# Recurrent blocks of a graph network: TensorE's order of sums, transposes and gate products within a group

## The chip, the cores and the metric

The kernel runs on one core of a Trainium2 chip. The metric is the device time of one execution in microseconds; the time before is the median of three runs. The profile shows one further execution, whose times are those of the hardware profiler.

## What is computed

The program is a network of four graph layers over 3125 nodes (padded to 3200, 25 tiles of 128) and 100000 edges. The change touches the third layer alone, four recurrent blocks one after the other:

```python
for b in range(4):
    x = h * norm_src[:, None]
    agg = segment_sum(x[src], dst, num_segments=n)
    g = agg * norm_dst[:, None] @ gcn_w[b] + gcn_b[b]
    gi = g @ gru_w_ih[b].T + gru_b_ih[b]
    i_r, i_z, i_n = split(gi, 3, axis=-1)
    h_r, h_z, h_n = split(gru_b_hh[b], 3)
    r = sigmoid(i_r + h_r)
    z = sigmoid(i_z + h_z)
    h = relu((1.0 - z) * tanh(i_n + r * h_n))
```

After the last block its input is added and each row is normalized.

## The kernel before

`gru_block` (from line 1395) makes one block. A matrix AT of edge counts between nodes, in bf16, stays in SBUF; the sum over neighbours is a product of the node features with it. At the start of a block `Split` loads the features in five pieces, scales them and writes them as three bf16 parts each (ScalarE and VectorE in turns).

The nodes are then handled in NG = 5 groups of GT = 5 tiles, 640 columns, each in two halves of HW = 320 columns. For each group, TensorE's loop does in this order (lines 1442 to 1457):

- it waits until VectorE has taken the rows of the prior group out of the two banks `pa` (semaphore `taken`);
- it sums the neighbours of half 0 into `pa[0]` and of half 1 into `pa[1]`: `sum_neighbours`, 25 tiles x 3 parts = 75 matmuls of 320 columns each (line 350);
- per half it multiplies the scaled sums by the weights `wg` into `pg[2]` (line 1448, f32), once VectorE has scaled them (line 1491, `sums_out`);
- it waits until ScalarE has added the bias to both halves (line 1466, `convs_out`) and makes six gate products, three gates x two halves, into the six banks `pg` (line 1452, f32);
- it waits for the state and transposes it, five f32 transposes into `pa` (line 1456).

ScalarE makes the bias, the sigmoids of the reset gate and of the keep gate (lines 1469 and 1472) and the tanh (line 1474). VectorE scales the sums, mixes reset gate and candidate (line 1498), makes the state (line 1502) and copies the transposed rows into `r_y` (line 1513; in the last block line 1515 adds the residual and the norm follows, with a square root on ScalarE, line 1477). SyncE stores `r_y` (line 1435) and, in the last block, loads the residual into it first (line 1433). All four engines run loops over the five groups. Each engine works its queue in order, and the semaphores say what it waits for. In the profile an f32 product stands as two records.

Of the kernel before, what the change touches and what calls it, by code (L numbers as in the profile page):

```python
# [12 lines left out]
P = 128  # L13
# [18 lines left out]
GT = 5  # L32
NG = NT // GT
GW = GT * P
HW = GW // 2
# [8 lines left out]
ALU = mybir.AluOpType  # L44
ACT = mybir.ActivationFunctionType
AX_X = mybir.AxisListType.X
ds = bass.ds
# [296 lines left out]
def sum_neighbours(pe, AT, parts, banks, f, g, half, lo):  # L344

    for j in range(NT):
        if half == 0 and j % GT == 0:
            pe.wait_ge(lo, f * NG + j // GT + 1)
        for k in range(SPLIT):
            mm = pe.matmul(banks, parts[:, k, j, f * P:(f + 1) * P], AT[:, j, ds(g * GW + half * HW, HW)],  # L350
                           start=(j == 0 and k == 0), stop=(j == NT - 1 and k == SPLIT - 1))
    return mm
# [1039 lines left out]
GATES = 3  # L1392


def gru_block(nc, K, D, AT, b, source, from_scale, to_scale, parts, target, residual):

    with ExitStack() as ctx:
        m = Mem(nc, ctx)
        wg = m.sb("r_wg", [P, P])
# [6 lines left out]
        summed, conv, reset, keep, cand = (work[:, i, :] for i in range(NG))  # L1406
        split = Split(m, source, 1, parts, [work[:, i, :].rearrange("p (t c) -> p t c", c=P) for i in range(NG)], from_scale)
# [3 lines left out]
        pa = [m.ps(f"r_pa{i}", [P, BANK]) for i in range(2)]  # L1411
        pg = [[m.ps(f"r_pg{c}{i}", [P, BANK]) for i in range(2)] for c in range(GATES)]
# [5 lines left out]
        halves = [slice(i * HW, (i + 1) * HW) for i in range(2)]  # L1418
        with nc.Block() as block:
            @block.sync  # L1420
            def _(sp):
                sp.sem_inc(stored, 16)
                for i in range(NG):
                    split.load(sp, i)
                sp.dma_start(wg[:, :], D["gcn_w"][b * P:(b + 1) * P, :]).then_inc(weights, 16)
                sp.dma_start(wi[:, :], D["gru_w"][b * P:(b + 1) * P, :]).then_inc(weights, 16)
                sp.dma_start(bg[:, :], D["gcn_b"][b * P:(b + 1) * P, :]).then_inc(weights, 16)
                sp.dma_start(bi[:, :], D["gru_bi"][b * P:(b + 1) * P, :]).then_inc(weights, 16)
                sp.dma_start(bh[:, :], D["gru_bh"][b * P:(b + 1) * P, :]).then_inc(weights, 16)
                with sp.Fori(0, NG) as g:  # L1430
                    if residual is not None:
                        sp.wait_ge(stored, g * 16 + 16)
                        sp.dma_start(y[:, :, :], rows(residual, g * GT, GT)).then_inc(resid, 16)
                    sp.wait_ge(done, g + 1)
                    sp.dma_start(rows(target, g * GT, GT), y[:, :, :]).then_inc(stored, 16)
                sp.wait_ge(stored, 16 * NG + 16)

            @block.tensor
            def _(pe):
                pe.sem_inc(turned, 1)  # L1440
                pe.wait_ge(weights, 80)
                with pe.Fori(0, NG) as g:
                    pe.wait_ge(taken, g * GT + 1)
                    for i in range(2):
                        sum_neighbours(pe, AT, parts, pa[i][:, 0:HW], 0, g, i, split.lo).then_inc(sums, 1)
                    for i in range(2):
                        pe.wait_ge(sums_out, g * 2 + i + 1)
                        pe.matmul(pg[2][i][:, 0:HW], wg[:, :], summed[:, halves[i]], start=True, stop=True).then_inc(convs, 1)
                    pe.wait_ge(convs_out, g * 2 + 2)
                    for c in range(GATES):  # L1450
                        for i in range(2):
                            pe.matmul(pg[c][i][:, 0:HW], wi[:, c * P:(c + 1) * P], conv[:, halves[i]],
                                      start=True, stop=True).then_inc(gates, 1)
                    pe.wait_ge(state, g + 1)
                    for u in range(GT):
                        pe.transpose(pa[u // 4][:, u % 4 * P:(u % 4 + 1) * P], cand[:, u * P:(u + 1) * P],
                                     K["identf"][:, :]).then_inc(turned, 1)

            @block.scalar
            def _(act):  # L1460
                split.scalar(act)
                act.wait_ge(biases, 1)
                with act.Fori(0, NG) as g:
                    for i in range(2):
                        act.wait_ge(convs, g * 2 + i + 1)
                        act.activation(conv[:, halves[i]], pg[2][i][:, 0:HW], ACT.Identity, bias=bg[:, 0:1]).then_inc(convs_out, 1)
                    for i in range(2):
                        act.wait_ge(gates, g * 6 + i + 1)
                        act.activation(reset[:, halves[i]], pg[0][i][:, 0:HW], ACT.Sigmoid, bias=brz[:, 0:1]).then_inc(gates_out, 1)
                    for i in range(2):  # L1470
                        act.wait_ge(gates, g * 6 + 3 + i)
                        act.activation(keep[:, halves[i]], pg[1][i][:, 0:HW], ACT.Sigmoid, bias=brz[:, 1:2], scale=-1.0).then_inc(gates_out, 1)
                    act.wait_ge(mixed, g * 2 + 2)
                    act.activation(cand[:, :], cand[:, :], ACT.Tanh, bias=bi[:, 2:3]).then_inc(tanned, 1)
                    if residual is not None:
                        act.wait_ge(var, g + 1)
                        act.activation(mv[:, :, 1], mv[:, :, 1], ACT.Sqrt).then_inc(dev, 1)

            @block.vector
            def _(dve):  # L1480
                dve.sem_inc(taken, 1)
                split.vector(dve)
                dve.wait_ge(weights, 80)
                dve.tensor_tensor(brz[:, :], bi[:, 0:2], bh[:, 0:2], ALU.add)
                dve.drain()
                dve.tensor_scalar(brz[:, 1:2], brz[:, 1:2], -1.0, None, ALU.mult)
                dve.drain().then_inc(biases, 1)
                with dve.Fori(0, NG) as g:
                    for i in range(2):
                        dve.wait_ge(sums, g * 2 + i + 1)  # L1490
                        dve.tensor_tensor(summed[:, halves[i]], pa[i][:, 0:HW], to_scale[:, ds(g * GW + i * HW, HW)],
                                          ALU.mult).then_inc(sums_out, 1)
                    dve.drain()
                    dve.wait_ge(turned, g * GT + 1)
                    for i in range(2):
                        dve.wait_ge(gates_out, g * 4 + i + 1)
                        dve.wait_ge(gates, g * 6 + 5 + i)
                        dve.scalar_tensor_tensor(out=cand[:, halves[i]], in0=reset[:, halves[i]], scalar=bh[:, 2:3],
                                                 in1=pg[2][i][:, 0:HW], op0=ALU.mult, op1=ALU.add).then_inc(mixed, 1)
                    dve.wait_ge(gates_out, g * 4 + 4)  # L1500
                    dve.wait_ge(tanned, g + 1)
                    dve.scalar_tensor_tensor(out=cand[:, :], in0=cand[:, :], scalar=0.0, in1=keep[:, :],
                                             op0=ALU.max, op1=ALU.mult).then_inc(state, 1)
                    if residual is None:
                        dve.wait_ge(stored, g * 16 + 16)
                    else:
                        dve.wait_ge(resid, g * 16 + 16)
                    for u in range(GT):
                        if u in (0, 4):
                            dve.wait_ge(turned, g * GT + min(u + 4, GT) + 1)  # L1510
                        result = pa[u // 4][:, u % 4 * P:(u % 4 + 1) * P]
                        if residual is None:
                            dve.tensor_copy(y[:, u, :], result).then_inc(taken, 1)
                        else:
                            dve.tensor_tensor(y[:, u, :], result, y[:, u, :], ALU.add).then_inc(taken, 1)
                    if residual is not None:
                        dve.drain()
                        norm_stats(dve, y, stats, mv, GT).then_inc(var, 1)
                        dve.wait_ge(dev, g + 1)
                        norm_apply(dve, y, mv, GT)  # L1520
                    dve.drain()
                    dve.sem_inc(done, 1)


RBF = 64
# [580 lines left out]
```

## Time and profile before

| what | us |
|---|---|
| median of 3 runs | 6668.77 (6667.44 to 6669.37) |
| the profiled execution | 6675.19 |
| its span | 6673.6 |
| TensorE busy in the span | 4334.3 |
| four blocks, first sums to last copy | 161.7, 162.3, 163.3, 161.7 |

The profiled execution lies 6.4 us above the median. A row of the timeline gives start, length, engine, line, operation, the tiles written and read, the number of instructions merged, and in brackets the idle time before and who ended it. The ends of matmuls are modelled, so that a matmul's length reaches into the next one's time: what a stream of them costs is read from start to start. The granted clock (PEclk) is 1.00 at 2.4 GHz and 0.50 at 1.2 GHz.

### The profile page before, as it was taken

The page shows a single profiled execution, that of the slowest core. Times are in us where ns is not written, and L with a number is a line of the kernel's source. Part 1 is how long each engine was busy: PE and PEld are TensorE (multiplying, and loading weights), DVE is VectorE, ACT ScalarE, POOL GpSimd, SP SyncE. Part 2 cuts the span into 40 slices and gives each one's busy share as a digit, 9 for nine tenths or more (in the row PEclk, how much of TensorE's full clock was granted, in tenths as well). Part 3 has the DMA queues.
Part 4 walks back from the last instruction along what each step waited for, and adds up shares of the span by engine and source line. Part 5 has one row for each costly group of instructions (what it writes and reads, how often), then busy time and mean ns, then how long its engine had stood idle before and what let it go on. Part 6 is the DMA issues. An engine that isn't in the chain of part 4 may idle for free. (4 is left out here: it accounts for less than half of the span.)

```text
span 6673.6 us, 101944 instructions
## 1 busy us (share of the span) xinstructions
PE 4334.3 (65%) x26966; PEld 3026.4 (45%) x26967; DVE 3767.7 (56%) x8412; ACT 1205.4 (18%) x2011; POOL 3659.2 (55%) x3721
## 2 busy tenths in 40 slices
PE   0666667186267777775466666641888778778774
PEld 0111114154156566553355555531555556556653
DVE  8777771054589898988466666662111244444443
ACT  0111111011211111111212211110211222222221
POOL 1666664600277777772477777735000057777771
PEclk9999998598589899987577777766998888888886
DMA  4111114110244444443233333353000123222344
GB/s 198 41 44 44 41 44 177 46 33 15 64 127 116 123 122 121 117 123 75 74 81 80 79 80 83 82 114 130 11 18 21 31 64 75 74 75 74 75 71 42
DMA packets 309188, 518.20 MB, mean 78 GB/s; under 512 B 105621, under 2 KB 221727, under 8 KB 298934
## 3 DMA queue, kind: packets, MB, share of 16 engines
q0 software_dynamic: 131616, 291.86, 18.6%
q1 hardware_dynamic: 177430, 224.82, 10.3%
q8 instruction: 43, 0.70, 0.0%
q14 instruction: 99, 0.81, 0.0%
HBM read 412.95 MB, written 103.45 MB: 77 GB/s over the span
## 5 line engine op out<-in xcount | busy, mean ns | idle before, releaser
L1017 POOL DMA_INDIRECT e_ring<-att_rows,e_near x1792 | 1841.6, 1028 | 550.2 <-issue 484.2
L1770 POOL DMA_INDIRECT e_nodes<-x,e_edges x880 | 884.2, 1005 | 311.5 <-issue 274.5
L1084 PE MATMUL e_psum<-e_ring,e_whole_pick 128*128 128x264 f32 (+1 forms) x3584 | 849.5, 390 | 297.8 <-DVE e_ring L1244 288.8
L1084 PEld LDWEIGHTS e_psum<-e_ring,e_whole_pick 128*128 128x128 f32 x3584 | 649.4, 225 | 423.5 <-issue 195.7
L1039 PE MATMUL e_px<-t_parts,e_pick 128*128 x5376 | 692.9, 270 | 118.1 <-DVE e_prod L1162 56.3
L1162 DVE TENSOR_TENSOR e_prod<-e_px,e_ring 128x512 f32<-128x512 f32 x672 | 458.3, 682 | 495.9 <-DMA e_ring<-att_rows,e_near 413.3
L1688 POOL DMA_INDIRECT sorted<-bx_held,bx_index x550 | 545.0, 991 | 251.3 <-issue 248.9
L280 PE MATMUL b_acc<-b_pick_key,b_pick_lo 128*128 128x416 bf16 (+1 forms) x1960 | 504.4, 346 | 176.5 <-DVE b_pick_key L251 159.5
L350 PE MATMUL r_pa<-gru_counts,gru_parts 128*128 x3000 | 448.7, 316 | 187.3 <-DMA r_bh<-in_gru_bh 169.6
L1039 PEld LDWEIGHTS e_px<-t_parts,e_pick 128*128 128x128 bf16 x5376 | 452.6, 107 | 210.2 <-issue 139.5
L1126 ACT ACTIVATE e_whole_pick<-e_pturn 128x512 f32<-128x512 bf16 x448 | 266.5, 595 | 1324.8 <-PE e_pturn L1075 1280.5
L251 DVE TENSOR_SCALAR b_pick_key<-b_lane,b_base,b_keyf 128x800 bf16<-128x800 int16 x980 | 487.4, 497 | 0.0
L1806 PE MATMUL e_pa<-e_msg,e_pick 128*128 128x128 f32 x1768 | 315.6, 333 | 249.4 <-DVEq L1864 248.4
L1806 PEld LDWEIGHTS e_pa<-e_msg,e_pick 128*128 128x128 f32 x1768 | 264.4, 229 | 435.4 <-DVEq L1864 420.4
L350 PEld LDWEIGHTS r_pa<-gru_counts,gru_parts 128*128 128x128 bf16 x3000 | 306.7, 103 | 328.9 <-issue 193.5
L1152 DVE TENSOR_REDUCE e_dots<-e_prod 128x8 f32<-128x512 f32 (+1 forms) x672 | 453.0, 674 | 0.0
L350 PE MATMUL g_pa<-gin_counts,g_parts 128*128 x2250 | 319.6, 306 | 191.8 <-ACT g_parts L316 160.6
L1244 DVE TENSOR_TENSOR e_ring<-e_ring 128x1024 f32<-128x1024 f32 (+1 forms) x448 | 423.7, 946 | 23.7 <-issue 23.7
L250 DVE TENSOR_SCALAR b_pick_lo<-b_lane,b_lof 128x128 bf16<-128x128 int16 x980 | 264.6, 270 | 239.1 <-PE b_acc L280 194.8
L1761 POOL IOTA e_lane<- 128x128 f32 x1 | 0.2, 237 | 712.2 <-ACTq L1822 712.2
L1863 DVE TENSOR_TENSOR e_msg<-e_msg,e_nodes 128x512 f32<-128x512 f32 x220 | 153.7, 699 | 397.3 <-DMA e_nodes<-x,e_edges 395.9
L280 PEld LDWEIGHTS b_acc<-b_pick_key,b_pick_lo 128*128 128x128 bf16 x1960 | 121.5, 98 | 543.5 <-DVE b_pick_key L251 527.7
(335 smaller groups left out, 6579.9 us busy)
## 6 DMA issues: line engine op xcount, KB each, us to landing
e_relb<-place SPq DMA_DIRECT2D x56, 1024.0 KB
sorted<-o_fill SPq DMA_DIRECT2D x13, 2244.0 KB, 34.3
e_edges<-sorted SPq DMA_DIRECT2D x221, 132.0 KB
e_ring<-att_rows,e_near POOLq DMA_INDIRECT x1792
kept<-gin_counts SPq DMA_DIRECT2D x5, 4000.0 KB, 33.5
gru_counts<-kept SPq DMA_DIRECT2D x5, 4000.0 KB
bx_held<-in_edge_rows POOLq DMA_DIRECT2D x51, 363.0 KB
e_nodes<-x,e_edges POOLq DMA_INDIRECT x880
```

Of the source, the lines that this page charges most:

```text
L251: dve.tensor_scalar(pick_key[:, b, :], lane[:, :], base[:, ds(w, 1)], keyf[:, ds(c, 1)], ALU.add, ALU.is_equal).then_inc(picked, 1)
L280: mm = pe.matmul(acc[q % 2][:, h, 0:z - a], pick_lo[:, b, :], pick_key[:, b, a:z], start=False, stop=False, skip_group_check=True)
L350: mm = pe.matmul(banks, parts[:, k, j, f * P:(f + 1) * P], AT[:, j, ds(g * GW + half * HW, HW)], start=(j == 0 and k == 0), stop=(j == NT ...
L1017: pool.indirect_dma_start(out=ring[:, s, r, 0:wd + HEADS], out_offset=None, in_=xrows, in_offset=bass.IndirectOffsetOnAxis(ap=near[:, s, r ...
L1039: mm = pe.matmul(px[g % 2][:, x * wd:(x + 1) * wd], pick[:, 1 - s, r, :], parts[:, n, ds(t, 1), :].rearrange("p o c -> p (o c)"), start=(n ...
L1084: mm = pe.matmul(psum[q % 2][:, 0:RING], whole_pick[:, q % 2, c, :], ring[:, s, q * G + c, :], start=(c == 0), stop=(c == G - 1))
L1152: dve.tensor_reduce(dots[:, s, :, g * XB:(g + 1) * XB].rearrange("p h x -> p x h"), prod[:, g % 4, :].rearrange("p (x h c) -> p x h c", x= ...
L1162: dve.tensor_tensor(prod[:, g % 4, :].rearrange("p (x c) -> p x c", x=XB), px[g % 2][:, :].rearrange("p (x c) -> p x c", x=XB), ring[:, 1 ...
L1244: dve.tensor_tensor(rows_, rows_, ring[:, s, q * G:(q + 1) * G, wd:wd + HEADS].unsqueeze(3).broadcast_to([P, G, HEADS, ch]), ALU.mult).the ...
L1688: pool.indirect_dma_start(out=self.D["sorted"], in_=self.held[s][:, u, :], in_offset=None, out_offset=bass.IndirectOffsetOnAxis(ap=self.in ...
L1770: pool.indirect_dma_start(out=nodes[:, s, u, :], out_offset=None, in_=source, in_offset=bass.IndirectOffsetOnAxis(ap=edges[:, q, u, RBF + ...
L1806: mm = pe.matmul(pa[s][:, 0:P], pick[:, s, u, :], msg[:, s, u, :], start=(u == 0), stop=(u == SUB - 1))
```

## The change

TensorE's loop is put in another order. It sums half 0 of group g; transposes the state of group g-1 (`turn`), now into the two banks of `pg[0]`; multiplies half 0 by `wg`; sums half 1; multiplies half 1; waits until the rows of group g-1 are taken; then it makes the three gate products of half 0 and the three of half 1, each half after its own bias. In the first group `turn` works on a state that does not exist yet and whose result nobody reads; after the loop a last `turn` follows. ScalarE makes the sigmoids in the order reset 0, keep 0, reset 1, keep 1. VectorE's loop is written out for the five groups: scaling of half 0, the rows of the prior group (with the norm in the last block), scaling of half 1, then mixing and state.

```diff
                 with pe.Fori(0, NG) as g:
+                    sum_neighbours(pe, AT, parts, pa[0][:, 0:HW], 0, g, 0, split.lo).then_inc(sums, 1)
+                    turn(g - 1)
+                    convolve(g, 0)
+                    sum_neighbours(pe, AT, parts, pa[1][:, 0:HW], 0, g, 1, split.lo).then_inc(sums, 1)
+                    convolve(g, 1)
                     pe.wait_ge(taken, g * GT + 1)
                     for i in range(2):
-                        sum_neighbours(pe, AT, parts, pa[i][:, 0:HW], 0, g, i, split.lo).then_inc(sums, 1)
-                    for i in range(2):
-                        pe.wait_ge(sums_out, g * 2 + i + 1)
-                        pe.matmul(pg[2][i][:, 0:HW], wg[:, :], summed[:, halves[i]], start=True, stop=True).then_inc(convs, 1)
-                    pe.wait_ge(convs_out, g * 2 + 2)
-                    for c in range(GATES):
-                        for i in range(2):
+                        pe.wait_ge(convs_out, g * 2 + i + 1)
+                        for c in range(GATES):
                             pe.matmul(pg[c][i][:, 0:HW], wi[:, c * P:(c + 1) * P], conv[:, halves[i]],
                                       start=True, stop=True).then_inc(gates, 1)
-                    pe.wait_ge(state, g + 1)
-                    for u in range(GT):
-                        pe.transpose(pa[u // 4][:, u % 4 * P:(u % 4 + 1) * P], cand[:, u * P:(u + 1) * P],
-                                     K["identf"][:, :]).then_inc(turned, 1)
+                turn(NG - 1)
```

The two functions that it calls:

```python
def turn(g):
    pe.wait_ge(state, g + 2)
    for u in range(GT):
        pe.transpose(pg[0][u // 4][:, u % 4 * P:(u % 4 + 1) * P], cand[:, u * P:(u + 1) * P],
                     K["identf"][:, :]).then_inc(turned, 1)

def convolve(g, i):
    pe.wait_ge(sums_out, g * 2 + i + 1)
    pe.matmul(pg[2][i][:, 0:HW], wg[:, :], summed[:, halves[i]], start=True, stop=True).then_inc(convs, 1)
```

ScalarE:

```diff
                     for i in range(2):
-                        act.wait_ge(gates, g * 6 + i + 1)
+                        act.wait_ge(gates, g * 6 + i * GATES + 1)
                         act.activation(reset[:, halves[i]], pg[0][i][:, 0:HW], ACT.Sigmoid, ...)
-                    for i in range(2):
-                        act.wait_ge(gates, g * 6 + 3 + i)
+                        act.wait_ge(gates, g * 6 + i * GATES + 2)
                         act.activation(keep[:, halves[i]], pg[1][i][:, 0:HW], ACT.Sigmoid, ...)
```

VectorE, whose steps are otherwise those of before, put into three functions:

```diff
-                with dve.Fori(0, NG) as g:
...
+                dve.sem_inc(state, 1)
+                for g in range(NG):
+                    scale_sums(g, 0)
+                    if g:
+                        take_rows(g - 1)
+                    scale_sums(g, 1)
+                    make_state(g)
+                take_rows(NG - 1)
```

`take_rows` reads `pg[0]` instead of `pa`. The loads, the splitting, the stores and the end of a block are as they were.

## Rows read from the trace of the kernel before

**Rows 1.** The page: the span, and the group of the sums' matmuls.
```profile
span 6673.6 us, 101944 instructions
...
L350 PE MATMUL r_pa<-gru_counts,gru_parts 128*128 x3000 | 448.7, 316 | 187.3 <-DMA r_bh<-in_gru_bh 169.6
```

**Rows 2.** Busy time by window, one for each of the four blocks.
```profile
core 0: us, PE busy (x) PEld busy (x) DVE busy (x) ACT busy (x) POOL busy (x), PEclk, DMA share, GB/s
4670.30:4832.00 161.70, 140.69 (x855) 93.90 (x855) 26.72 (x61) 38.13 (x55) 0.00 (x0) 0.92 0.03 8
4845.90:5008.20 162.30, 141.18 (x855) 94.02 (x855) 26.08 (x60) 26.41 (x44) 0.00 (x0) 0.92 0.03 8
5022.20:5185.50 163.30, 142.20 (x855) 94.19 (x855) 25.92 (x60) 26.28 (x44) 0.00 (x0) 0.92 0.03 8
5199.40:5361.10 161.70, 140.69 (x855) 93.92 (x855) 39.53 (x129) 45.19 (x64) 0.00 (x0) 0.92 0.06 16
```

**Rows 3.** Timeline, first group of the first block, to the next sums.
```profile
4670.35 21.89 PE L350 MATMUL r_pa<-gru_counts,gru_parts 128*128 x150 [124.95 <-DMA r_bh<-in_gru_bh]
...
4682.19 0.49 DVE L1491 TENSOR_TENSOR r_work<-r_pa,to_scale 128x320 f32<-128x320 f32 x1 [4.00 <-PE r_pa L350]
...
4692.07 0.70 PE L1448 MATMUL r_pg<-r_work,r_wg 128*128 128x320 f32 x2
4692.38 0.49 DVE L1491 TENSOR_TENSOR r_work<-r_pa,to_scale 128x320 f32<-128x320 f32 x1 [9.70 <-PE r_pa L350]
...
4692.93 0.81 PE L1448 MATMUL r_pg<-r_work,r_wg 128*128 128x320 f32 x2 [0.16 <-DVE r_work L1491]
...
4694.31 1.28 ACT L1469 ACT_TABLE_LOAD   x1
...
4694.35 3.50 PE L1452 MATMUL r_pg<-r_work,r_wi 128*128 128x320 f32 x12 [0.62 <-ACT r_work L1466]
4695.61 0.94 ACT L1469 ACTIVATE r_work<-r_pg,r_brz 128x320 f32<-128x320 f32 x2
...
4697.35 1.09 DVE L1498 SCALAR_TENSOR_TENSOR r_work<-r_work,r_bh,r_pg 128x320 f32<-128x320 f32 x2 [4.47 <-PE r_pg L1452]
4698.47 0.83 ACT L1474 ACTIVATE r_work<-r_work,r_bi 128x640 f32<-128x640 f32 x1 [1.08 <-DVE r_work L1498]
...
4699.33 0.83 DVE L1502 SCALAR_TENSOR_TENSOR r_work<-r_work 128x640 f32<-128x640 f32 x1 [0.90 <-ACT r_work L1474]
...
4700.21 1.17 PE L1456 MATMUL r_pa<-identf,r_work 128*128 128x128 f32 x5 [2.36 <-DVE r_work L1502]
4701.20 1.08 DVE L1513 COPY r_y<-r_pa 128x128 f32<-128x128 f32 x5 [1.05 <-PE r_pa L1456]
...
4702.43 22.89 PE L350 MATMUL r_pa<-gru_counts,gru_parts 128*128 x150 [1.05 <-DVE r_y L1513]
```

**Rows 4.** Windows of 1 us in that group; columns as in rows 2.
```profile
4697.00:4698.00 1.00, 0.85 (x4) 0.26 (x2) 0.65 (x2) 0.39 (x1) 0.00 (x0) 1.00 0.00 0
...
4699.00:4700.00 1.00, 0.00 (x0) 0.00 (x0) 0.67 (x1) 0.98 (x2) 0.00 (x0) 1.00 0.00 0
...
4701.00:4702.00 1.00, 0.38 (x2) 0.00 (x0) 0.80 (x4) 0.00 (x0) 0.00 (x0) 0.50 0.00 0
```

**Rows 5.** Timeline of TensorE, second group's end, and the last block's groups.
```profile
4733.31 0.77 PE L1456 MATMUL r_pa<-identf,r_work 128*128 128x128 f32 x5 [2.36 <-DVE r_work L1502]
4735.23 21.87 PE L350 MATMUL r_pa<-gru_counts,gru_parts 128*128 x150 [1.15 <-DVE r_y L1513]
...
5199.43 21.88 PE L350 MATMUL r_pa<-gru_counts,gru_parts 128*128 x150 [14.91 <-DMA r_bh<-in_gru_bh]
...
5329.17 21.86 PE L350 MATMUL r_pa<-gru_counts,gru_parts 128*128 x150 [1.15 <-DVE r_y L1515]
```

**Rows 6.** Timeline of SyncE, second load of the residual; DMA issues: KB, us to landing.
```profile
5238.08 0.39 SPq L1433 DMA_DIRECT2D r_y<-x  x1
...
state<-r_y SPq DMA_DIRECT2D x15, 320.0 KB, 2.5
```

More of the change, by code:

```diff
@@ L1441, in _ @@
                 pe.wait_ge(weights, 80)
-                with pe.Fori(0, NG) as g:
+                def turn(g):
+                    pe.wait_ge(state, g + 2)
+                    for u in range(GT):
+                        pe.transpose(pg[0][u // 4][:, u % 4 * P:(u % 4 + 1) * P], cand[:, u * P:(u + 1) * P],
+                                     K["identf"][:, :]).then_inc(turned, 1)
+                def convolve(g, i):
+                    pe.wait_ge(sums_out, g * 2 + i + 1)
+                    pe.matmul(pg[2][i][:, 0:HW], wg[:, :], summed[:, halves[i]], start=True, stop=True).then_inc(convs, 1)
+                with pe.Fori(0, NG) as g:
+                    sum_neighbours(pe, AT, parts, pa[0][:, 0:HW], 0, g, 0, split.lo).then_inc(sums, 1)
[3 more added lines that the diff above has]
+                    convolve(g, 1)
                     pe.wait_ge(taken, g * GT + 1)
                     for i in range(2):
-                        sum_neighbours(pe, AT, parts, pa[i][:, 0:HW], 0, g, i, split.lo).then_inc(sums, 1)
-                    for i in range(2):
-                        pe.wait_ge(sums_out, g * 2 + i + 1)
-                        pe.matmul(pg[2][i][:, 0:HW], wg[:, :], summed[:, halves[i]], start=True, stop=True).then_inc(convs, 1)
-                    pe.wait_ge(convs_out, g * 2 + 2)
-                    for c in range(GATES):
-                        for i in range(2):
+                        pe.wait_ge(convs_out, g * 2 + i + 1)
+                        for c in range(GATES):
                             pe.matmul(pg[c][i][:, 0:HW], wi[:, c * P:(c + 1) * P], conv[:, halves[i]],
                                       start=True, stop=True).then_inc(gates, 1)
-                    pe.wait_ge(state, g + 1)
-                    for u in range(GT):
-                        pe.transpose(pa[u // 4][:, u % 4 * P:(u % 4 + 1) * P], cand[:, u * P:(u + 1) * P],
-                                     K["identf"][:, :]).then_inc(turned, 1)
+                turn(NG - 1)
             @block.scalar
@@ L1487, in _, with scale_sums, make_state @@
                 dve.drain().then_inc(biases, 1)
-                with dve.Fori(0, NG) as g:
-                    for i in range(2):
[L1490 to L1497, printed above, removed]
+                def scale_sums(g, i):
+                    dve.wait_ge(sums, g * 2 + i + 1)
+                    dve.tensor_tensor(summed[:, halves[i]], pa[i][:, 0:HW], to_scale[:, g * GW + i * HW:g * GW + (i + 1) * HW],
+                                      ALU.mult).then_inc(sums_out, 1)
+                def make_state(g):
+                    for i in range(2):
+                        dve.wait_ge(gates_out, g * 4 + i * 2 + 1)
+                        dve.wait_ge(gates, g * 6 + (i + 1) * GATES)
                         dve.scalar_tensor_tensor(out=cand[:, halves[i]], in0=reset[:, halves[i]], scalar=bh[:, 2:3],
@@ L1503, in _, with take_rows @@
                                              op0=ALU.max, op1=ALU.mult).then_inc(state, 1)
[L1504 to L1507, printed above, removed]
+                def take_rows(g):
+                    dve.wait_ge(stored if residual is None else resid, g * 16 + 16)
                     for u in range(GT):
                         if u in (0, 4):
-                            dve.wait_ge(turned, g * GT + min(u + 4, GT) + 1)
-                        result = pa[u // 4][:, u % 4 * P:(u % 4 + 1) * P]
+                            dve.wait_ge(turned, (g + 1) * GT + min(u + 4, GT) + 1)
+                        result = pg[0][u // 4][:, u % 4 * P:(u % 4 + 1) * P]
                         if residual is None:
```

## The prediction, made before the change was run

> **What bounds the kernel now.** The table of windows over the four recurrent blocks comes first [rows 2]: each lasts 161.7 to 163.3 us, 649.0 us together, a tenth of the span, and TensorE is busy for 141 of each 162 us while VectorE has 26 to 40 and ScalarE 26 to 45. So TensorE is the bound and what can be won is its 21 us of idle time per block, plus what a low clock costs it. The page says what the busy part is: 3000 neighbour matmuls [rows 1], 150 per group, 20 groups. Next the timeline of one group [rows 3], read as one chain in which each step starts a moment after the one before ends. Sums (150 matmuls); scaling of half 1 on VectorE from 4692.38; product with wg from 4692.93; bias on ScalarE, until the gates may start; a table load to 4695.59; gate products 4694.35 to 4697.85; sigmoids; mixing on VectorE to 4698.44; tanh; state to 4700.16; transposes; five copies to 4702.28; next sums at 4702.43. Nothing of the next group's sums runs in this stretch, although they need only the parts made at the start of the block. Last, the granted clock [rows 4]: 1.00 (2.4 GHz) while the gates run and still at 4699 to 4700, with TensorE idle; 0.50 (1.2 GHz) at 4701 to 4702 and into the next sums. The rest of the program neither overlaps the blocks nor changes.
>
> **Unit prices.** One warm half of the sums, 75 matmuls, is the distance of the two scalings in [rows 3]: 4692.38 - 4682.19 = 10.19 us, so 20.38 us for a group. The rows of a whole group's sums say 21.89, 22.89, 21.87 [rows 3, 5]; an all-warm one would show 20.38 + 0.17 of modelled end = 20.55. So 1.3 to 2.3 us per group is the low clock after the pause. The scaling round trip: TensorE is free to go on at 4692.07 (it starts the product of half 0 then) and starts the next one at 4692.93, so 0.86 us. Gate products: 12 records in 3.50 us, the last of 0.43, hence (3.50 - 0.43)/11 = 0.279 us each, two for a product: 0.56 us a product, 3.35 us for six. Five transposes: 0.77 us warm, 1.17 us at the low clock, modelled end of about 0.3 included [rows 3, 5], so TensorE is held for some 0.6 us.
>
> **The change, part by part.** (1) The sums of half 0 of group g+1 stand ahead of the transposes of group g. They take 10.2 us. The remaining chain of group g needs less: from the product of half 1 (call its start C) to the state it took 4700.16 - 4692.93 = 7.2 us before, of which 3.9 us are now the gates themselves. So the wait for the state is over about 7 us before TensorE arrives at it, and sigmoids, mixing, tanh and state cost nothing. (2) The transposes go behind half 0 and in front of its product with wg, which has to wait 0.86 us for the scaling anyway. Their 0.6 us lie in that wait. Cost 0; without this cover 0.6 us. (3) The product of half 0, 0.56 us, was hidden behind the scaling of half 1; now it stands in the open. (4) The scaling of half 1 has nothing beside it any more: 0.86 us, then 0.56 us of product. (5) The gates go by halves. Those of half 0 need the bias of half 0, ready since 9 us, and start at once instead of 1.42 us after C. Those of half 1 need the bias of half 1, ready at C + 1.42 (4694.35 - 4692.93), while TensorE comes to them at C + 0.56 + 1.67 = C + 2.2. No wait is left, and the gates end at C + 3.91. (6) The copies into r_y (1.08 us, with the last block's norm about 5 us) run under half 1 of the sums, 10.2 us. The gates' new wait for them is long met. VectorE's scaling of half 1 is now queued behind the copies; it is not due until 10.2 us after the scaling of half 0, and 0.9 + 5 us stand before it: cover of 4 us in the last block, 8 in the others. The copies wait for the store of the earlier group. In the last block the reload of r_y is issued at 5238.08, some 25 us ahead of its use, and a store of the same 320 KB took 2.5 us to land [rows 6]: hidden behind a group of over 26 us. In that block ScalarE also holds the square root ahead of the next bias of half 0, some 3 us late, needed 10 us later: hidden. (7) Transposes write the banks of the reset gate instead of the sums' banks, so sums and copies share none. (8) Five more transposes in each block, of nothing useful, in the first group: they lie in the same 0.86 us. (9) VectorE's loop is written out five times; more code, off the path, 0 to 1 us in all.
>
> **New period.** 20.38 + (0.86 + 0.56) + (0.86 + 0.56) + 3.35 = 26.57 us, against (5329.17 - 5199.43)/4 = 32.44 us [rows 5]. **Last group of a block**: up to C 20.38 + 1.42 + 0.86 = 22.66 us. After C nothing overlaps, but the order within is better. ScalarE's table load ends at C + 2.68 as before; sigmoids of 0.42 us pitch in the order reset 0, keep 0, reset 1, so reset 1 ends at C + 4.0; the last gate product ends at C + 4.06; the second mixing ends at C + 4.65 instead of C + 5.51. The copies ended at C + 9.35 before and so end at C + 8.49. Sum 31.15 us. **A block**: 4 x 26.57 + 31.15 = 137.43, plus the low clock of its first sums, 1.3 to 2.3, taken as 1.9 since every block starts after a pause of 15 us: 139.3 us. Before, the mean of [rows 2] was 162.25. The gain is 22.9 us a block, 91.7 in four. The third block was slower than the others at the same clock share (163.3), which I take to stay: minus 1.4. **Gain 90.3 us.** The profiled execution took 6675.2 us (span 6673.6); it should become 6584.9. It lay 6.4 us above the median of the runs, so the forecast for the median is 6668.8 - 90.3 = 6578.5 us.
>
> **Where it hangs on the clock.** In all 20 groups the clock held through the scaling wait, the bias wait of 0.62 us and the gates (the row of twelve records in 3.50 us stands for 20 alike), and fell only after the idle 2.36 us ahead of the transposes [rows 3, 4]. After the change the longest pause between two groups' work inside a block is 0.86 us. So the low clock goes from 16 of 20 groups. The Trainium skill, "TensorE: Matmul & The Clock Gate", part 4 on PE-mode transposes, speaks against putting transposes there: it says that full clock does not engage for them, and gives around 275 ns each. In this trace five take 0.77 us together at a clock of 1.00, so the measurement decides; by the page's figure they would outlast the scaling wait by an estimated 0.5 us, 10 us in all.
>
> **The rivals.** *The clock still falls once per group*, since TensorE's work is now chopped by two waits and by transposes. Price, 16 groups x the 1.3 to 2.3 us of today = 30 us: 6608 us. Against it: the clock held through a longer broken stretch before (4692 to 4698). Chance 0.07. *The loop's back edge is exposed.* Before, it lay under the wait for the copies: between the transposes from 4733.31 and the sums at 4735.23 at most 1.4 us beside transposes [rows 5]. Now gates are directly ahead of it. TensorE's sequencer is released for the second half of the gates at C + 1.42 and the array works until C + 3.91, so 2.5 us cover it if the sequencer runs ahead; if not, up to 1.4 us x 16 = 23 us: 6602 us. The Trainium skill, "Runtime: NRT & Kernel Launch", on instruction fetch mechanics, says that a taken branch out of the fetch window stalls for a fetch; the body of more than 340 instructions makes that likely here, and it is this rival. Chance 0.08. *Slower:* the clock never rises within a block, because its pauses now come every 11 us and not every 32. A matmul then takes twice 0.136 us and a group loses 20.4 us. The change saves 32.44 - 26.57 = 5.87 us a group, so it loses from 5.87/0.136 = 43 of 150 sums at the low clock, which is 12 us of each group (now 10 to 17 matmuls). At all 150, 20 x 20.4 = 408 us on top of the forecast makes about 6985 us. For it: only that before there were 20 unbroken us; against it: the clock rose within the time that twice the loss of 1.3 to 2.3 us makes, 3 to 5 us into each group's sums. Chance 0.02. *It does not do what it says*, a wait in the old place (for the state, the copies or the store) still ends last each group: the time stays within 0.2%. Against it: the covers of 4 to 8 us above. Chance 0.02. The forecast keeps 0.81, with its own range of 6570 to 6590: each of the forty pauses of 0.86 us may be 0.2 us shorter or 0.3 us longer.
>
> **Range and chances.** The range takes in the forecast's and reaches towards both partial rivals: 6566 to 6603. Faster by over 0.2% (13 us, about what a measurement of this kernel can tell): 0.81 + 0.07 + 0.08 = 0.96; same 0.02; slower 0.02.
>
> **What would show it.** In the new profile a group's sums should start every 26.6 us; each half 10.2 us at clock 1.00 from the second group on; transposes a moment after half 0, waiting for nothing; TensorE idle only before each product with wg, 0.2 to 0.3 us in the middle and about 0.7 at the end; gates following without a wait, and the next sums right behind them; a block from first sums to last copies 139 us, TensorE idle in it for some 10 us instead of 21. Sums rows still over 10.5 us a half would mean the clock; a wait "issue" ahead of each group's sums would mean the back edge; a wait of the transposes for the state, or of the gates for the copies, would mean that the chain is not hidden.

## The result and the profile after

The changed kernel took 6574.8 us (median of 4 runs, 6567.95 to 6577.49), the kernel before 6669.07 beside it: ratio 0.9855, 95% interval 0.9841 to 0.9868, 94 us or 1.4% faster. The forecast was 6578.5 us, a gain of 90.3.

Busy time by window of the changed kernel, one window for each of the four blocks, columns as in [rows 2], which it answers:

```profile
core 0: us, PE busy (x) PEld busy (x) DVE busy (x) ACT busy (x) POOL busy (x), PEclk, DMA share, GB/s
4666.20:4804.20 138.00, 131.70 (x860) 92.16 (x860) 26.59 (x60) 38.26 (x55) 0.00 (x0) 0.98 0.03 10
4818.00:4956.70 138.70, 131.98 (x860) 92.09 (x860) 26.45 (x61) 26.67 (x45) 0.00 (x0) 0.98 0.03 10
4970.50:5109.70 139.20, 132.55 (x860) 92.33 (x860) 26.27 (x61) 26.57 (x44) 0.00 (x0) 0.98 0.03 10
5123.80:5263.20 139.40, 132.70 (x860) 92.40 (x860) 39.69 (x129) 45.32 (x64) 0.00 (x0) 0.98 0.07 19
```

From the first sums to the end of the last copy the blocks took 138.27, 138.66, 139.23 and 139.38 us, 555.5 together against 649.0: 93.5 of the 94 us are here. Two things moved, and both can be read off. TensorE's busy time fell by 8.0 to 9.7 us a block, for the same sums and products (and five more transposes), at a mean clock of 0.98 instead of 0.92; and the window less the busy time went from 21 us to under 7.

The timeline of the changed kernel, from the end of the first group's sums to the second group's product of half 1 (it answers [rows 3]; L1446 are the transposes, L1451 the product with wg, L1463 the gates, L1498 the scaling, L1509 the state, L1519 the copies):

```profile
4689.57 0.49 DVE L1498 TENSOR_TENSOR r_work<-r_pa,to_scale 128x320 f32<-128x320 f32 x1 [11.09 <-PE r_pa L350]
...
4690.11 0.81 PE L1451 MATMUL r_pg<-r_work,r_wg 128*128 128x320 f32 x2 [0.58 <-DVE r_work L1498]
...
4690.76 3.39 PE L1463 MATMUL r_pg<-r_work,r_wi 128*128 128x320 f32 x12
...
4693.99 10.35 PE L350 MATMUL r_pa<-gru_counts,gru_parts 128*128 x75
...
4695.78 0.82 DVE L1509 SCALAR_TENSOR_TENSOR r_work<-r_work 128x640 f32<-128x640 f32 x1 [0.97 <-ACT r_work L1481]
...
4704.18 0.71 PE L1446 MATMUL r_pg<-identf,r_work 128*128 128x128 f32 x5
4704.38 0.49 DVE L1498 TENSOR_TENSOR r_work<-r_pa,to_scale 128x320 f32<-128x320 f32 x1 [7.77 <-PE r_pa L350]
4704.88 1.08 DVE L1519 COPY r_y<-r_pg 128x128 f32<-128x128 f32 x5
...
4704.92 0.81 PE L1451 MATMUL r_pg<-r_work,r_wg 128*128 128x320 f32 x2
...
4705.56 10.35 PE L350 MATMUL r_pa<-gru_counts,gru_parts 128*128 x75
...
4716.50 0.81 PE L1451 MATMUL r_pg<-r_work,r_wg 128*128 128x320 f32 x2 [0.58 <-DVE r_work L1498]
```

The next sums stand right behind the gates (4693.99), the state is ready at 4696.60 and the transposes come to it at 4704.18 with no idle time in their brackets: 7.6 us lie between. One idle stretch is left in a group, the 0.58 us for the scaling of half 1. VectorE's loop, written out, also has no drain and no wait ahead of the mixing any more; before, VectorE sat idle for 4.47 us ahead of it [rows 3], so they cost nothing there. The next group repeats it: sums at 4693.99 and at 4720.37, a period of 26.38 us.

### The profile page after: what moved, and what is told of

The parts are those of the page before. It is cut to its first block and busy times, and to the rows that moved or that the text cites. A ratio compares the mean times of both kernels' runs of the same rounds, so it can differ in the third digit from the quotient of the medians.

```text
span 6571.6 us, 101744 instructions
## 1 busy us (share of the span) xinstructions
PE 4297.5 (65%) x26986; PEld 3031.9 (46%) x26987; DVE 3770.1 (57%) x8412; ACT 1205.3 (18%) x2011; POOL 3658.1 (56%) x3721
## 5 line engine op out<-in xcount | busy, mean ns | idle before, releaser
L1084 PE MATMUL e_psum<-e_ring,e_whole_pick 128*128 128x264 f32 (+1 forms) x3584 | 869.4, 397 | 293.0 <-DVE e_ring L1244 284.9
L1084 PEld LDWEIGHTS e_psum<-e_ring,e_whole_pick 128*128 128x128 f32 x3584 | 667.8, 231 | 418.0 <-issue 191.9
L350 PE MATMUL r_pa<-gru_counts,gru_parts 128*128 x3000 | 423.4, 304 | 169.5 <-DMA r_bh<-in_gru_bh 169.5
L350 PEld LDWEIGHTS g_pa<-gin_counts,g_parts 128*128 128x128 bf16 x2250 | 221.3, 99 | 290.3 <-issue 201.7
```

Of the source, the lines that this page charges most:

```text
L1084: mm = pe.matmul(psum[q % 2][:, 0:RING], whole_pick[:, q % 2, c, :], ring[:, s, q * G + c, :], start=(c == 0), stop=(c == G - 1))
```

## The experiments

All kernels share everything outside the blocks, so each has two measures: the median, and the four blocks by its trace, from the first sums to the last copy. The blocks come from one profiled execution, the medians from other executions too. The median less the blocks should be one number, and is, within the scatter of runs:

| kernel | median us | blocks us | difference |
|---|---|---|---|
| before | 6669.1 | 649.0 | 6020.1 |
| changed | 6574.8 | 555.5 | 6019.3 |
| before, filled | 6636.3 | 617.5 | 6018.8 |
| changed, gates by gate | 6593.6 | 571.6 | 6022.0 |
| before, gates by half | 6649.0 | 629.2 | 6019.8 |
| products inside the sums | 6558.2 | 533.1 | 6025.1 |
| chain plus 4 us | 6590.3 | 572.3 | 6018.0 |
| chain plus 10 us | 6664.7 | 639.2 | 6025.5 |
| transposes after half 1 | 6612.4 | 589.1 | 6023.3 |

The medians scatter by some 5 us, the blocks of one kernel by about 1.

**How much was the clock?** Before, TensorE filled:

```diff
+                    for _k in range(16):
+                        pe.matmul(pa[0][:, 0:HW], parts[:, 0, 0, 0:P], AT[:, 0, 0:HW], start=True, stop=True)
                     pe.wait_ge(state, g + 1)
                     for u in range(GT):
                         pe.transpose(pa[u // 4][:, u % 4 * P:(u % 4 + 1) * P], cand[:, u * P:(u + 1) * P], ...)
+                    for _k in range(10):
+                        pe.matmul(pg[0][0][:, 0:HW], parts[:, 0, 0, 0:P], AT[:, 0, 0:HW], start=True, stop=True)
```

> The kernel before, with TensorE kept busy in its two idle stretches of each group: 16 spare matmuls of 320 columns into pa[0] ahead of the wait for the state, 10 into pg[0][0] ahead of the wait for the copies (some 2.2 and 1.4 us at full clock). Nothing else is moved. It asks how much of the gain was the clock and how much the overlap. My account (of 5.87 us a group, 1.3 to 2.3 us were the clock): the granted clock stays at 1.00 in 16 of 20 groups, the group's period falls from 32.4 to about 30.6 us, the four blocks from 649.0 to about 618 us together, the median by about 31 us to 6638. The rival, that the clock was most of the gain: 60 us or more, below 6610. A third, that spare work delays the copies or the next sums: no gain, 6669 or more.

6636.31 us (6633.45 to 6637.6), blocks 617.5. Timeline of TensorE in this kernel, first group's end and the next two groups' sums (L1455 and L1461 are the spare matmuls):

```profile
4691.96 2.34 PE L1455 MATMUL r_pa<-gru_counts,gru_parts 128*128 128x320 bf16 x16
4694.48 0.77 PE L1458 MATMUL r_pa<-identf,r_work 128*128 128x128 f32 x5 [0.19 <-DVE r_work L1506]
4695.09 1.52 PE L1461 MATMUL r_pg<-gru_counts,gru_parts 128*128 128x320 bf16 x10
4696.45 20.54 PE L350 MATMUL r_pa<-gru_counts,gru_parts 128*128 x150
...
4726.93 20.54 PE L350 MATMUL r_pa<-gru_counts,gru_parts 128*128 x150
```

With work in the pauses every group's sums after the first take 20.54 us, not 21.9 or 22.9 [rows 3, 5], and the period is 30.48. The chain of each group is as long as before, and yet 31.5 us of the 93.5 are there. A third of the gain is what filling the pauses alone gives, and that is the clock.

**Gates by halves.** Undone in the changed kernel, and alone in the old one:

```diff
-                    for i in range(2):
-                        pe.wait_ge(convs_out, g * 2 + i + 1)
-                        for c in range(GATES):
+                    pe.wait_ge(convs_out, g * 2 + 2)
+                    for c in range(GATES):
+                        for i in range(2):
```

(with the waits of ScalarE and VectorE to match; the second kernel has the same lines the other way round).

> The changed kernel with one part undone: the six gate products again gate by gate, after the bias of both halves, and ScalarE's and VectorE's waits to match. My account: the gates start 1.42 us after the second product with wg instead of 0.64, so 0.8 us idle in each group and a mixing that ends later: period from 26.4 to about 27.2 us, blocks from 555.5 to about 571.5 us together, the median about 16 us above the changed kernel's, 6591. The rival, that halves only move work inside a stretch that something else bounds: no difference within 4 us.

> The kernel before with that part alone: gates by halves, each half after its own bias; sums and transposes where they were. My account: everything after the second product with wg comes 0.8 to 0.9 us earlier, blocks from 649.0 to about 632 us, the median by about 17 us to 6652. If gates by halves need the new order to pay (since ScalarE's table load bounds the sigmoids in the old chain): within 4 us of before.

Undone: 6593.64 us (6593.0 to 6597.66), blocks 571.6. Alone: 6649.04 us (6640.16 to 6657.26; ratio 0.9968, interval 0.9958 to 0.9978), blocks 629.2. TensorE's timeline with the part undone:

```profile
4692.86 0.81 PE L1451 MATMUL r_pg<-r_work,r_wg 128*128 128x320 f32 x2 [0.58 <-DVE r_work L1499]
4694.37 3.47 PE L1463 MATMUL r_pg<-r_work,r_wi 128*128 128x320 f32 x12 [0.71 <-ACT r_work L1474]
```

The wait of 0.71 us for the bias is back, 16.1 us in 20 groups. In the old order the part is worth 19.8 us by the blocks. TensorE's timeline of that kernel, first group:

```profile
4688.48 0.70 PE L1448 MATMUL r_pg<-r_work,r_wg 128*128 128x320 f32 x2
...
4689.98 3.39 PE L1452 MATMUL r_pg<-r_work,r_wi 128*128 128x320 f32 x12
...
4695.84 0.77 PE L1456 MATMUL r_pa<-identf,r_work 128*128 128x128 f32 x5 [2.47 <-DVE r_work L1501]
```

The gates start 1.50 us after the product of half 0 and not 2.28 (4692.07 to 4694.35 in [rows 3]), 15.6 us in 20 groups; from there to the transposes 1.1 us less is spent in all. The other 3.0 us lie between the transposes and what follows them, and they are the clock: five transposes take 0.77 us in all 20 groups here, while before it was 1.17 in one group and 0.77 in the next [rows 3, 5]. The part pays in either order.

**Is the chain really hidden, and how far?** After the tanh ScalarE copies the tile onto itself, 5 times in one kernel and 12 in the other:

```diff
-                    act.activation(cand[:, :], cand[:, :], ACT.Tanh, bias=bi[:, 2:3]).then_inc(tanned, 1)
+                    act.activation(cand[:, :], cand[:, :], ACT.Tanh, bias=bi[:, 2:3])
+                    for _k in range(5):
+                        act.drain()
+                        again = act.activation(cand[:, :], cand[:, :], ACT.Copy)
+                    again.then_inc(tanned, 1)
```

> The changed kernel with the hidden chain made longer: after the tanh ScalarE copies cand onto itself 5 times (some 0.83 us each, with a drain before each, 4.5 us in all). It asks whether the chain from the gates to the state is really covered, and by how much. My account: in the changed kernel the state is ready 7.5 us before the transposes start, so the period stays at 26.4 us in all groups and only the end of each block, where nothing covers the chain, grows by 4.5 us: 18 us in all, blocks from 555.5 to about 574 us, 6593. The rival, that the chain ends each group (a wait took the place of the old one): 4.5 us in each of 20 groups, 90 us, 6665.

> The same with 12 copies, 10.7 us, which is more than the cover of 7.5 us. My account: TensorE now waits some 3.1 us for the state after half 0, period about 29.4 us with the clock at 1.00 throughout; 16 x 3.1 + 4 x 10.7 = 92 us, 6667. If a pause of that length inside a group is enough for the clock to fall, as it fell in the old order after 2.36 us of idle time, transposes and 1.05 us more, another 1.3 to 2.3 us in each group: period 30.7 to 31.7 us, 6690 to 6705. If the cover were larger than the trace says: period 26.4, only the ends, 6618.

With 5 copies (one row, 3.96 us for the five): 6590.3 us (two runs, 6583.29 and 6597.31), blocks 572.3, that is 16.7 us more, 4.2 for each block's end, and the period is 26.38 as without them. TensorE's sums in two groups, half 0 each:

```profile
4687.44 10.35 PE L350 MATMUL r_pa<-gru_counts,gru_parts 128*128 x75
4697.63 0.71 PE L1446 MATMUL r_pg<-identf,r_work 128*128 128x128 f32 x5
...
4713.83 10.35 PE L350 MATMUL r_pa<-gru_counts,gru_parts 128*128 x75
```

With 12 copies (9.58 us): 6664.7 us (6657.45 to 6669.94), blocks 639.2, near the kernel before again. TensorE's timeline over two groups:

```profile
4702.63 0.77 PE L1446 MATMUL r_pg<-identf,r_work 128*128 128x128 f32 x5 [1.99 <-DVE r_work L1513]
4703.23 0.72 PE L1451 MATMUL r_pg<-r_work,r_wg 128*128 128x320 f32 x2
4703.77 12.03 PE L350 MATMUL r_pa<-gru_counts,gru_parts 128*128 x75
...
4732.58 0.76 PE L1446 MATMUL r_pg<-identf,r_work 128*128 128x128 f32 x5 [1.97 <-DVE r_work L1513]
4733.18 0.70 PE L1451 MATMUL r_pg<-r_work,r_wg 128*128 128x320 f32 x2
4733.72 10.35 PE L350 MATMUL r_pa<-gru_counts,gru_parts 128*128 x75
```

and windows of 1 us in it:

```profile
4701.00:4702.00 1.00, 0.00 (x0) 0.00 (x0) 0.25 (x1) 0.98 (x2) 0.00 (x0) 1.00 0.00 0
...
4704.00:4705.00 1.00, 1.00 (x5) 0.61 (x4) 0.47 (x3) 0.52 (x1) 0.00 (x0) 0.50 0.00 0
...
4731.00:4732.00 1.00, 0.00 (x0) 0.00 (x0) 0.30 (x1) 0.98 (x2) 0.00 (x0) 1.00 0.00 0
...
4734.00:4735.00 1.00, 1.00 (x10) 0.73 (x8) 0.42 (x3) 0.45 (x1) 0.00 (x0) 1.00 0.00 0
```

So the cover ends between 4 and 10 us, as the 7.5 us read from the trace said, and with 12 copies TensorE sat idle for 1.96 to 1.99 us in 15 of the 16 exposed groups (2.34 in one), 9.58 less some 7.6. The exposed part was 1.9 us (a period of 28.28 where the clock held, 4720.25 to 4748.53) where 3.1 was expected: a copy with its drain took 0.80 us, not 0.89. The two expectations for the clock both came true, in turn, in 8 of the 16 exposed groups each: the same idle 2 us was followed by a clock of 0.50 in one group (half 1 of the sums 12.03 us, period 29.96) and not in the next (10.35). Behind the state VectorE also scales half 0 late, at 4702.49, since its queue holds the state's instruction ahead of the scaling.

**Does the place of the transposes matter?** They go behind half 1:

```diff
-                    turn(g - 1)
                     convolve(g, 0)
                     sum_neighbours(pe, AT, parts, pa[1][:, 0:HW], 0, g, 1, split.lo).then_inc(sums, 1)
+                    turn(g - 1)
                     convolve(g, 1)
...
-                    if g:
-                        take_rows(g - 1)
                     scale_sums(g, 1)
+                    if g:
+                        take_rows(g - 1)
```

> The changed kernel with the transposes put into the other pause, behind half 1 and ahead of its product with wg; VectorE takes the rows after scaling half 1. It asks whether the place of the transposes matters or only that the chain is hidden. My account: both pauses stay 0.75 us, but the gates of half 0 need the bank that the transposes wrote, and so wait for the copies: 0.7 us more in each group of the first three blocks (period 27.1), and in the last block also for the bias of half 0, which stands on ScalarE behind the square root of the norm, some 4 us more (period 30 to 31). Blocks from 555.5 to about 582 us, 6600. The rival, that any pause will do: within 4 us of 6575.

6612.44 us (two runs, 6607.35 and 6617.54), blocks 140.9, 140.4, 140.0 and 167.9, together 589.1. In TensorE's timeline, a group of the first block and one of the last:

```profile
4714.17 0.81 PE L1451 MATMUL r_pg<-r_work,r_wg 128*128 128x320 f32 x2
4715.27 3.50 PE L1463 MATMUL r_pg<-r_work,r_wi 128*128 128x320 f32 x12 [0.29 <-DVE r_y L1519]
...
5177.72 0.81 PE L1451 MATMUL r_pg<-r_work,r_wg 128*128 128x320 f32 x2
5183.04 5.14 PE L1463 MATMUL r_pg<-r_work,r_wi 128*128 128x320 f32 x12 [4.51 <-ACT r_work L1474]
```

The gates wait for the copies, 0.29 us each time, and the period in the first three blocks is 26.94 us (27.1 expected). In the last block they wait 4.5 us for a bias that stands on ScalarE behind the square root. The clock falls at the end of that pause or within it, so the gates, 3.4 to 3.5 us elsewhere, take 5.14 to 6.32; that is why the last block's period is 33 to 34 us and not the 30 to 31 expected. The clock's windows in that group of the last block, where it is still at 1.00 late in the pause (the next group's pause already has windows at 0.50, 5214 to 5216):

```profile
5182.00:5183.00 1.00, 0.00 (x0) 0.00 (x0) 0.64 (x3) 0.99 (x3) 0.00 (x0) 1.00 0.00 0
...
5184.00:5185.00 1.00, 1.00 (x3) 0.61 (x3) 0.00 (x0) 0.99 (x2) 0.00 (x0) 0.50 0.84 245
...
5187.00:5188.00 1.00, 1.00 (x5) 0.61 (x4) 0.22 (x1) 0.84 (x2) 0.00 (x0) 1.00 0.89 268
```

So the place is worth 33.6 us of the 93.5, over a third: in the changed kernel the copies and the norm have the whole of half 1 for cover, here they have almost nothing.

**The last pause.** The products with wg go into the sums, which are written tile by tile (`add_tiles` makes the sums of some of the 25 tiles, `make_gates` the six gate products as before; their definitions and the loop that they replace are left out here):

```diff
...
+                add_tiles(0, 0, 0, NT)
+                turn(-1)
+                add_tiles(0, 1, 0, 3)
+                convolve(0, 0)
+                add_tiles(0, 1, 3, NT)
+                with pe.Fori(1, NG) as g:
+                    add_tiles(g, 0, 0, 3)
+                    convolve(g - 1, 1)
+                    add_tiles(g, 0, 3, 8)
+                    make_gates(g - 1)
+                    add_tiles(g, 0, 8, NT)
+                    turn(g - 1)
+                    add_tiles(g, 1, 0, 3)
+                    convolve(g, 0)
+                    add_tiles(g, 1, 3, NT)
+                convolve(NG - 1, 1)
+                make_gates(NG - 1)
+                turn(NG - 1)
```

> A step beyond the change: the pauses of 0.75 us for the scaling are filled too. The product with wg of half 0 goes behind the first 3 tiles of the sums of half 1, that of half 1 behind the first 3 tiles of the next group's half 0, the gates behind tile 8, the transposes between the halves. My account (what is left in a group is one open pause of 0.75 and 0.15 of another): period from 26.38 to about 25.5 us, blocks from 555.5 to about 541 us, the median by about 15 us to 6560. The rival, that f32 products set between bf16 sums cost TensorE a switch of their own, or that the state is late for transposes that now have only 17 tiles (6.9 us) of cover: no gain, or slower by up to 10 us.

6558.17 us (6553.15 to 6559.07), blocks 533.1, 8 us less than the 541 expected. One group of TensorE's timeline, without any idle time (L1458 are the sums, L1468 the gates):

```profile
4697.81 0.70 PE L1451 MATMUL r_pg<-r_work,r_wg 128*128 128x320 f32 x2
4698.35 2.20 PE L1458 MATMUL r_pa<-gru_counts,gru_parts 128*128 x15
4700.39 3.39 PE L1468 MATMUL r_pg<-r_work,r_wi 128*128 128x320 f32 x12
4703.62 7.09 PE L1458 MATMUL r_pa<-gru_counts,gru_parts 128*128 x51
4710.54 0.71 PE L1446 MATMUL r_pg<-identf,r_work 128*128 128x128 f32 x5
4711.09 1.39 PE L1458 MATMUL r_pa<-gru_counts,gru_parts 128*128 x9
4712.31 0.70 PE L1451 MATMUL r_pg<-r_work,r_wg 128*128 128x320 f32 x2
4712.85 10.35 PE L1458 MATMUL r_pa<-gru_counts,gru_parts 128*128 x75
4723.04 0.70 PE L1451 MATMUL r_pg<-r_work,r_wg 128*128 128x320 f32 x2
```

The period is 25.23 us (4697.81 to 4723.04), 0.25 less than expected, because a product ahead of which nothing waits costs 0.54 us and one behind a wait 0.64 (4697.81 to 4698.35 here; 4690.11 to 4690.76 in the changed kernel). That is 4 us of the 8; the rest lies in the first and last groups of the blocks, which the account of 16 groups left out. No cost for setting f32 products between the sums is to be seen: from start to start the 15 matmuls take 2.04 us, the 51 take 6.92 and the 9 take 1.22, 0.136 us each, as in an unbroken half (10.19/75). To see it beside the changed kernel both ran once more on one chip, with a third:

> The changed kernel once more, on the same chip as the next two, since its blocks and those of the kernel with the products inside the sums (533.1 us) differ by 22.4 us by the traces while the medians, taken on different occasions, differ by 17. Blocks 555.5 within 1 us, some 94 us below the kernel before.

> The kernel with the products inside the sums once more beside the changed kernel. If the blocks alone tell them apart: 22.4 us below the changed kernel, ratio to before about 0.9825. If time outside the blocks gives some back: 10 to 17 us.

The changed kernel: 6576.04 us (6573.92 to 6577.61), ratio 0.9855 (0.984 to 0.9871), blocks 554.7. Products inside: 6552.7 us (6550.44 to 6554.66), ratio 0.982 (0.9807 to 0.9833), blocks 532.5. The 23.3 us between them are those of the blocks (22.2), and the intervals are apart. This is the fastest version, 1.8% below the kernel before.

**The back edge:**

```diff
-                with pe.Fori(0, NG) as g:
+                for g in range(NG):
```

> The changed kernel with TensorE's loop over the groups written out five times, so that there is no back edge. It asks whether the back edge costs anything now that it lies directly behind the gates. My account: nothing, since the sums follow the gates after 3.23 us for six products both times: period 26.38, blocks 555.5, within 3 us of the changed kernel. If the back edge or its fetch is exposed by what the trace doesn't show as a gap: up to 1.4 us less in each of 16 groups, 22 us faster. If the longer code costs fetches: slower.

6578.63 us (6570.21 to 6580.93), blocks 555.4, ratio 0.9856: no difference. Its sums, too, start 3.23 us after the gates:

```profile
4695.57 3.39 PE L1463 MATMUL r_pg<-r_work,r_wi 128*128 128x320 f32 x12
4698.80 10.35 PE L350 MATMUL r_pa<-gru_counts,gru_parts 128*128 128x320 bf16 x75
```

The back edge costs nothing in the changed kernel.

## Why the prediction was right, and where it was off

- **What bounds the blocks, and what would be hidden:** right. Period 26.38 us against 26.57 predicted; the state's cover of 7.5 us (7 predicted) was tested by making the chain longer; copies, norm and reload run under half 1.
- **The clock goes to 1.00 in 16 of 20 groups:** right. Every half but the first of a block takes 10.35 us. The part given to the clock, 1.3 to 2.3 us a group, measured 1.96 with the filled pauses (32.44 - 30.48; the spare work itself cost some 0.04). The rival of a clock that falls once per group had the right mechanism and the wrong place: a pause of 0.75 us does not do it, one of 2 us does it in some groups.
- **Transposes under the scaling wait:** right. The product of half 0 starts 0.74 us after the first transpose does; ahead of the product of half 1, where nothing lies in the pause, it is 0.74 us too (4690.11, against sums that began at 4679.18 and last 10.19). The clock was at 1.00 throughout and five took 0.71 us. The prediction set the page of the Trainium skill ("TensorE: Matmul & The Clock Gate", part 4, around 275 ns each) against its own 0.77 us for five, and multiplied it by five. But the profile's own length of one transpose (f32 here, bf16 on the page) agrees with the page:

```profile
L1446 PE MATMUL r_pg<-identf,r_work x120: 272/273/478, 4677.8 to 5261.9; 128*128 128x128 f32 x120
```

  That is the length of one (ns: least, median, most), and they overlap: (0.71 - 0.27)/4 = 0.11 us from start to start at a clock of 1.00, and (1.33 - 0.48)/4 = 0.21 us where the clock was 0.50 (the last five of the first block). So the estimate of 0.5 us beyond the scaling wait took a length for a pitch; and the transposes did run at full clock when it was granted.
- **The back edge:** this rival did not come true, as the kernel with the loop written out shows. The figure of 1.4 us was only an upper bound from a place where it was itself hidden.
- **Terms that were off:** the scaling wait was sized at 0.86 us and is 0.75. The product follows the start of the scaling by 0.55 us as before; what differs is that VectorE starts the scaling 0.31 us after the sums are through in [rows 3] (4692.07 to 4692.38) and 0.20 us in the new trace (4689.37 to 4689.57). The 0.31 us stand in all three kernels whose VectorE runs a loop (before, filled, gates by half), the 0.20 us in all whose loop is written out. So the writing-out, put at 0 to 1 us and off the path in part 9, seems to be on it: 40 scalings of 0.11 us would be some 4 us, an estimate. No run changes VectorE's loop alone, so this is not shown. The product behind a wait costs 0.64 us and not 0.56; six gates 3.23 and not 3.35. Together 0.19 us less in each period, 3.0 us in 16 groups. The low clock of the first sums of a block was taken as 1.9 us and cost 1.4, 2.2, 2.8 and 3.0 (their half 0 took 11.74, 12.59, 13.15 and 13.31 us against 10.35), 1.8 us more in all. The slower third block, taken to stay, did not: its periods are 26.38 as elsewhere (4999.72 to 5026.10), so that its 1.4 us were the clock as well. A row of the third block before, against 21.87 in [rows 5]:

```profile
5055.52 22.15 PE L350 MATMUL r_pa<-gru_counts,gru_parts 128*128 x150 [1.16 <-DVE r_y L1513]
```

  The end of a block, product of half 1 to the last copy, was 8.4 us in three blocks and 8.8 in the first, against 8.49. Added up, 3.0 us in the periods, 0.6 in the last groups and 1.4 in the third block were gained beyond the forecast and 1.8 lost to the clock: the 3.2 us between 90.3 and 93.5. The errors partly cancel.
- **TensorE idle some 10 us a block:** under 7. The estimate counted the whole pauses, but the modelled end of the last matmul reaches 0.17 us into each, and the middle pause is filled by the transposes (0.04 us idle where 0.2 to 0.3 was expected).

The gain of 93.5 us by its parts: 31.5 are the clock (the filled kernel), 16.1 to 16.8 the gates by halves (undone; alone 19.8, less the 3.0 of clock that the 31.5 hold already), and the rest, some 45, the overlap of the chain with the next sums. The last is a difference, not a run of its own, and holds whatever the written-out loop of VectorE gives.

## What to carry to other kernels

Where an engine ends a group with a chain over other engines and the next group needs nothing of it, put a long piece of the next group ahead of the wait, and put what the chain returns into a pause that is there anyway, ahead of enough work to cover what follows from it; here the other pause would have lost a third of the gain. Read the cover off the trace (the time from the result being ready to its being asked for) and ask what else in each queue stands behind the waiting instruction. A gap in TensorE costs more than its length where the clock falls after it: here 1.96 of the 6.06 us that a period lost (32.44 to 26.38).

## What the runs showed of the hardware

An idle stretch of 2 us was followed by a granted clock of 0.50 in some groups and of 1.00 in others of the same kernel, with the same instructions around it. A bf16 accumulation stayed open over f32 products into other banks at no cost that the rows show: 0.136 us a matmul with and without them. Five f32 transposes of 128x128 in a stream started 0.11 us apart at a clock of 1.00 and 0.21 at 0.50, each with a length of 0.27 us at 1.00. An f32 product of 128x320 held TensorE for 0.54 us in a stream and 0.64 us as the first after a wait. At half clock the six gate products took up to 6.32 us instead of 3.39, and in the group shown the clock rose again while they ran, with f32 work alone (0.50 at 5184 to 5185, 1.00 at 5187 to 5188).
